# Scan of a Mamba-2 block: GpSimd's residual add and ScalarE's D·x of the first half change their places in the chunk

## What is computed

```python
    Y_diag = jnp.einsum('bcqhn,bcshn,bhcqs,bcshp->bcqhp', Cm, Bm, Lm, xdt)
    states = jnp.einsum('bcqhn,bhcq,bcqhp->bchpn', Bm, decay_states, xdt)
    ...
    Y_off = jnp.einsum('bcqhn,cbhpn,bhcq->bcqhp', Cm, prevs, jnp.exp(dAc))
...
    y = y + Dp[None, None, :, None] * x_h          # "D·x"
    y = rmsnorm(y * jax.nn.silu(z), norm_w)
    return y @ out_proj_w
...
h = residual + mamba2(h, ...)                      # then h2 = rmsnorm(h), the second norm
x = x + _L0_attn_ref(_layernorm(x), ...)           # the outer residual: x0 + h, kept as "xh"
```

## Time and profile before

| | |
|---|---|
| time, median of 3 runs | 1437.84 us (1435.71 to 1439.34) |
| the profiled execution | 1437.76 us, its span 1435.9 us |
| busy: PE, DVE, ACT, POOL | 1361.5, 889.7, 710.3, 438.3 us (95, 62, 49, 31% of the span) |
| the scan (`ssd`) | 274.0 to about 572.4 us |
| `diagonal(c, 0)` of chunk 1, 2 and 15 starts at | 303.55, 320.11 and 548.64 us |

### The profile page before, as it was taken

The page is one execution under the profiler, slowest core; times in us unless marked ns, Lnnn a source line. Parts: engine busy times, 40 slices in busy tenths (PEclk is TensorE's granted clock), DMA queues, the critical chain, the costliest instruction groups (busy, mean ns, idle before and its releaser), DMA issues.

```text
span 1435.9 us, 20597 instructions
## 1 busy us (share of the span) xinstructions
PE 1361.5 (95%) x7179; PEld 1095.8 (76%) x7179; DVE 889.7 (62%) x1279; ACT 710.3 (49%) x1313; POOL 438.3 (31%) x431
## 2 busy tenths in 40 slices
PE   6899999889999987999999999999999889999998
PEld 5677778656666665888888888888887689999997
DVE  7789788666666666233333333333236779999997
ACT  5445445677878775221211212121211358888886
POOL 2112121246666664210110101010101026556563
PEclk9999999999999999999999999999999979999999
DMA  6133123713333221510001000002034934434431
GB/s 207 60 117 118 60 88 140 220 52 109 116 115 117 104 102 56 189 30 15 30 15 29 29 15 29 15 29 96 1 110 137 334 95 70 80 70 76 72 48 23
DMA packets 69048, 122.63 MB, mean 85 GB/s; under 512 B 11743, under 2 KB 28127, under 8 KB 68960
## 3 DMA queue, kind: packets, MB, share of 16 engines
q1 hardware_dynamic: 59696, 103.67, 21.3%
q0 software_dynamic: 8736, 16.79, 6.8%
q10 hardware_dynamic: 528, 1.05, 0.2%
HBM read 81.37 MB, written 43.78 MB: 87 GB/s over the span
## 4 chain that ended last, share of the span: by engine, by line
PE 56%; DVE 2%; issue 1%; DMA 0%; ACT 0%; POOL 0%; DVEq 0%; POOLq 0%; ACTq 0%
PE fin_bank L1953 53%; PE fin_bank L2094 1%; PE fin_bank L2113 1%; DVE onehot L1862 0%; DMA xs<-xn_rows,idx 0%; PE fin_bank L2021 0%; PE fin_bank L2009 0%; DVE ff_w_lo L1754 0%; DMA out_dram<-result_rows,idx 0%; DVE fi_bn L1789 0%; ACT ff_w_hi L1623 0%; PE fin_bank L2086 0%; POOL out_dram L1577 0%; DVE oj L1857 0%; PE fin_bank L2019 0%
## 5 line engine op out<-in xcount | busy, mean ns | idle before, releaser
L1716 DVE TENSOR_TENSOR ff_prod<-ff_prod,fin_bank 128x512 f32<-128x512 f32 x64 | 44.0, 688 | 263.8 <-PE fin_bank L1953 263.8
L1953 PE MATMUL fin_bank<-ff_hT_hi,ff_w_hi 128*128 128x512 f32 x512 | 202.8, 396 | 3.2 <-DVE ff_w_lo L1724 3.2
L1953 PE MATMUL fin_bank<-ff_hT_lo,ff_w_hi 128*128 128x512 f32 x512 | 202.7, 396 | 0.0
L1953 PE MATMUL fin_bank<-ff_hT_hi,ff_w_lo 128*128 128x512 f32 x512 | 202.5, 395 | 0.0
L1507 POOL TENSOR_TENSOR ff_w_lo<-ff_stage,ff_w_hi 128x1024 fp32r<-128x1024 f32 (+1 forms) x24 | 56.5, 2356 | 411.3 <-ACT ff_w_hi L1613 406.3
L1598 ACT ACTIVATE ff_prod<-fin_bank 128x512 f32<-128x512 f32 x64 | 38.3, 598 | 230.6 <-PE fin_bank L1953 230.5
L687 PE MATMUL pj_bank<-hT_hi,w_in_hi 128*128 128x512 f32 x324 | 131.8, 407 | 5.8 <-DVE w_in_lo L587 5.0
L1601 ACT ACTIVATE ff_p_hi<-ff_prod 128x512 fp32r<-128x512 f32 x64 | 40.5, 633 | 190.4 <-DVE ff_prod L1716 190.4
L555 DVE SCALAR_TENSOR_TENSOR conv_acc<-raw,conv_w,conv_acc 128x512 f32<-128x512 f32 x144 | 108.1, 751 | 37.9 <-ACT raw L355 32.8
L687 PE MATMUL pj_bank<-hT_lo,w_in_hi 128*128 128x512 f32 x324 | 128.8, 398 | 0.0
L687 PE MATMUL pj_bank<-hT_hi,w_in_lo 128*128 128x512 f32 x324 | 128.2, 396 | 0.0
(11 more groups left out here) (301 smaller groups left out, 3095.1 us busy)
## 6 DMA issues: line engine op xcount, KB each, us to landing
cv_rows<-cst SPq DMA_DIRECT2D x12, 1024.0 KB, 4.2
cv<-cv_rows SPq DMA_DIRECT2D x16, 768.0 KB, 4.4
zs_rows<-zst SPq DMA_DIRECT2D x8, 1024.0 KB, 6.5
zs<-zs_rows SPq DMA_DIRECT2D x16, 512.0 KB, 5.3
wx<-in_L_ffn_Wg_dram SPq DMA_DIRECT2D x8, 704.0 KB, 8.1
wx<-in_L_ffn_Wu_dram SPq DMA_DIRECT2D x8, 704.0 KB, 8.9
x<-_attn_hidden_states_dram SPq DMA_DIRECT2D x16, 256.0 KB, 5.5
xh_rows<-x SPq DMA_DIRECT2D x16, 256.0 KB, 2.0
```

What stands on the lines that cost most here:

```text
L1716: eng.tensor_tensor(prod[c][:, :], prod[c][:, :], up_ps[c][:, :], ALU.mult).then_inc(s["prod"], 1)
L1953: mm = eng.matmul(ps, w[a], x[b], start=first and i == 0, stop=last and i == 2)
```

## The change

On GpSimd `residual(e)` moves, in turns 0 to 15, from behind `second_norm(e)` to right behind `row_scale(e)`, so that it stands in front of `scaled_x(c + 1)` and `second_norm(e)`; in the last turn it stays where it was. On ACT `skip_x(c, 0)`, four activations, moves from behind `high(e, 1)` to the front of the turn, ahead of `cum_exp(c, 0)`. No instruction, wait or buffer is added or taken away.

```diff
--- before.py
+++ after.py
@@ -918,11 +918,14 @@
                     decay_carry(c)
                 if e >= 0:
                     row_scale(e)
+                    if c < TILES:
+                        residual(e)
                 if c + 1 < TILES:
                     scaled_x(c + 1)
                 if e >= 0:
                     second_norm(e)
-                    residual(e)
+                    if c == TILES:
+                        residual(e)
 
         @block.scalar
         def _(eng):
@@ -1004,6 +1007,7 @@
                 e, f = c - 1, c - 2
                 now, late, later = c < TILES, 0 <= e < TILES, 0 <= f
                 if now:
+                    skip_x(c, 0)
                     cum_exp(c, 0)
                     exps(c, 1)
                 if c == 0:
@@ -1011,7 +1015,6 @@
                 if late:
                     high(e, 1)
                 if now:
-                    skip_x(c, 0)
                     mask(c, 1)
                     exps(c, 2)
                     mask(c, 2)
```

## The result

The changed kernel takes 1419.89 us in the median of 4 runs (1418.80 to 1421.11), the kernel before 1436.78 us (1435.19 to 1439.34); the ratio is 0.9881, with a 95% interval of 0.9863 to 0.9899. That is 16.9 us, 1.2%, faster; 15.5 us were predicted. The profiled execution took 1419.77 us, 18.0 less than the profiled one of before.

A forecast was written before the change was run, and what follows sets the result against it. TensorE bounds the scan, so only its waits can be won: 14.0 us over 13 chunks, plus 1.3 and 0.4 at the start, less 0.2 at the end, is 15.5; 1437.8 − 15.5 = 1422.3 us, range 1418.5 to 1432.0.

The forecast's parts named there:

- The bound and its two waits: Scan: TensorE is the bound; it waits for ACT's D·x (8.9 us) and the load of `cv` and `zs` (8.4 us).
- The residual in front: On POOL: residual ends at about 418.24, loads come 6 us earlier, all load waits go, 5.6 us won.
- predicted cover: Second norm on POOL ends by 424.8, ahead of `turn_h2` at about 425.2: 0.4 us to spare, cost nothing.
- D·x in front: On ACT, D·x ahead of `cum_exp(c, 0)`: `diagonal` no longer waits for it, gain 0.63 us in each chunk.
- slack: Chain gate, D·x, `cum_exp`, `cexp`, scores: the scores are there 0.3 us before `diagonal` needs them.
- The first rival: Scores late: hand-overs or `cexp` behind L903 make `diagonal` wait for scores; 1425 to 1432 us, 17%.
- The sum: Whole kernel: 14.0 us for 13 chunks, 1.3 for two further `diagonal` waits, 0.4 for chunk 0, less 0.2 at the end.
- One edit has no effect: Loads as late as now, D·x early: 15 × 0.63 + 0.4 = 9.9 us won, 1428 us; chance 5%.
- DVE behind two instructions of POOL: POOL goes from residual to `scaled_x` without letting yres in; chunk 18.1 us, 1444.6 us in all, slower; chance 8%.
- L903 holds DVE to its end: `cexp` on DVE waits for POOL's L903, 1.58 us; chunk 17.6 us, 1437 us in all, no gain but the start's; 6%.

The follow-up runs named there:

- the POOL edit alone: Kernel before with only the residual moved in front of `scaled_x` and the second norm, D·x where it was: 1431.6 us, ratio 0.9954.
- D·x alone: Kernel before with only D·x of the first half moved ahead of `cum_exp(c, 0)` on ACT, residual where it was: 1434.2 us, ratio 0.9975.
- the kernel with the loads first: Kernel before with D·x moved to the front and, on SP, loads of cv and zs ahead of the residual's wait and store: 1421.3 us, ratio 0.9887.

## Why the prediction was right, point by point

- **The bound and its two waits.** Right, and both gone. That `cexp` holds `carried` next and a chunk without load waits takes 17.15 us is shown by the POOL edit alone: 222.94 us against 222.95 predicted. But the 5.6 us above that base are not all load waits, as the prediction has it. 3.6 of them lie in one chunk, of 20.75 us, in which a store landed after 3.9 us instead of 2.0 (issued at 511.17, the loads at 515.07) and TensorE stood idle for 2.42; then it ran at 1.2 GHz, from 521.0 to 524.3 us. That chunk has 2.0 us more idle time and 1.6 us more busy time than the next one, which takes 17.15:

```profile
520.00:525.00 5.00, 4.17 (x36) 3.37 (x36) 1.46 (x3) 2.87 (x8) 2.05 (x2) 0.66 0.13 51
...
521.76 1.98 PE L1206 MATMUL ss_bank<-decay,xdt 128*64 128x128 f32 x16
```

- **The residual in front.** All times came as worked out, counted from D: residual's end 11.54 (predicted 11.54), yres's end 11.83 (11.83), the loads 13.59 (13.6). POOL was first, the worse side, which had been taken without a row that told which it would be. The second norm ends 0.57 us ahead of `turn_h2`; predicted cover 0.4.
- **D·x in front.** `cum_exp` starts at D + 13.71 (predicted 13.65), the scores end at 16.21 (16.17), `diagonal` starts at 16.46 (16.51). The gain of 0.65 to 0.7 us a chunk is right, the **slack is not**: 0.3 us on record, 0.10 measured. The step that gave it compared the end of the scores with the modelled end of `seg`; it left out the 0.15 us from the scores' end to `diagonal`, and that `diagonal` starts 0.07 ahead of `seg`'s end. The first rival (scores late, 17%) was nearer than it looked, and its two causes are shown: hand-overs that add up to 0.1 us more are enough, and the collision with L903 adds 0.33. That `diagonal` came when forecast, with so little to spare, is in part luck.
- **The sum.** 14.0 for the 13 chunks, 14.5 measured (16.45 instead of 16.5). Chunk 1: 0.65, measured 0.70. Start to `diagonal(1, 0)`: 0.4 + 0.65, measured 2.33; the sum has no term for the remaining 1.2, most of which goes with the clock. End: −0.2, measured −0.23 from `diagonal(15, 0)` on. 0.7 us of the 18.0 lie ahead of the scan, where both kernels are the same. Without those 0.7 the profiled executions differ by 17.3 us; what that is over 15.5 is mostly the start, and so, probably, is what the medians' 16.9 is over it.
- **One edit has no effect (5%, 1428).** The mechanism was told, the price was wrong: 9.9 us won for D·x alone, 3.6 measured (227.43 us for the 13 chunks; 1.6 of them are again TensorE at 1.2 GHz). The step added its 0.63 us a chunk as if the loads kept their distance to `diagonal`. They hang on `rows` of the chunk before, and that loop could be read from the trace of before: transposes that wait for a transfer at 414.80, and again 17.46 us later:

```profile
432.26 0.66 PE L1239 MATMUL ss_bank<-ident,cv 128*128 128x128 f32 x4 [0.70 <-DMA zs<-zs_rows]
```

- **DVE behind two instructions of POOL (8%).** It did not happen: in every chunk looked at `scaled_x` was put back by 0.19 us and yres let in.
- **L903 holds DVE to its end (6%).** It doesn't. In the changed kernel `cexp` is first (413.13 against 413.43), and L903 is the one that grows, to 1.83 us. Where `cexp` starts 0.22 us behind it (400.55 above), or `low` 0.22 in the earlier trace rows, both end 1.24 us behind L903's start, and so does the `cexp` that starts 0.33 behind (1.23, with the residual behind `scaled_x`). An estimate from that: DVE is kept out for the first 0.69 us of its 1.57 (1.24 less the 0.55 that `cexp` needs behind L904 in the earlier trace rows). The Trainium skill, "SBUF — State Buffer", section "SBUF: two separate sides", says that whichever of the two starts first has the pair for the whole instruction. The trace doesn't agree, and the measurement decides: with this form, one input and a scalar from SBUF, POOL doesn't keep it to the end.

## What to carry to other kernels

Before an edit is priced, look for loops that come round once a chunk over other engines and the transfers, and write down the length of each; a wait can be won only down to the second longest, and two edits on two loops of the same length are worth more together (14.5 us) than alone (1.1 and 5.6). Hang a load on what frees its buffer and on nothing else: with ACT's edit in place, the wait for the residual and its store in front of the loads of `cv` and `zs` cost 12.2 us of the 13 chunks (227.43 against 215.21). Slack is counted to the start of the waiting instruction with its hand-over, not to the end of the one ahead of it; 0.1 us was left here, and half a microsecond of new work on ACT took back more than half of the gain.

## What the runs showed of the hardware that was not expected

- A delay can cost more than its length, and a longer one hardly more: 0.52 us made a chunk 0.73 us longer and 0.94 us 0.84, as the first put DVE's `cexp` into the part of L903 that keeps it out and the second past it.
- POOL's scaling by a scalar (128x512, 1.57 us) keeps a DVE instruction with two SBUF inputs out for only about its first 0.69 us (an estimate, from above); the product of two SBUF tensors (L904) does to its end, and again in the kernel with the loads first (`cexp` done 0.55 us behind it).
- At a nearly equal start, POOL at 409.08 and DVE's yres at 409.11, POOL went first, in every chunk looked at; and where DVE was already waiting, it went ahead of POOL's next instruction.
- A wait of 2.42 us was followed by 3.3 us of TensorE at 1.2 GHz, which cost 1.6 us more.
